# Decoder layer on one core: expansion, normalization and routing as one pipeline over batches, places looked up by matmul

## The reference

```python
x = x + state_space(layernorm(x), ...)          # a scan over 256 tokens with 16 states
x = x + align(ctx, layernorm(x))                # warping path between ctx and x; each token of x
                                                # gets the sum of the ctx rows that its path meets
x = x + moe(layernorm(x), gate, w0, w1, wo)     # below

def moe(x, gate, w0, w1, wo):                   # 4096 tokens, 64 experts, two for each token
    weights, selected = top_k(x @ gate, 2);  weights = softmax(weights)
    order = argsort(selected.reshape(-1))       # 8192 entries, grouped by expert
    xs = x[order // 2]
    h = silu(ragged_dot(xs, w0, sizes)) * ragged_dot(xs, w1, sizes)
    out = ragged_dot(h, wo, sizes)
    return sum over the two entries of a token of out * weight
```

## Time and profile before

| | us |
|---|---|
| three runs | 1441.17, 1444.8, 1447.7; median 1444.8 |
| the profiled execution | 1447.63 |
| its span | 1445.9 |
| first loop of `expand` | 773.9 to 822.7 |
| scales | 822.7 to 828.0 |
| second loop | 828.0 to 863.9 |
| `route` | 863.9 to 941.7 |
| `experts` | 941.7 to 1405.0 |
| `combine` | 1405.0 to 1445.9 |

### The profile page before, as it was taken

The page is one execution under the profiler, slowest core; times in us unless marked ns, Lnnn a source line. Parts: engine busy times, 40 slices in busy tenths (PEclk is TensorE's granted clock), DMA queues, the critical chain, the costliest instruction groups (busy, mean ns, idle before and its releaser), DMA issues. The chain is left out here.

```text
span 1445.9 us, 20750 instructions
## 1 busy us (share of the span) xinstructions
PE 995.5 (69%) x6537; PEld 901.4 (62%) x6537; DVE 946.0 (65%) x1936; ACT 583.8 (40%) x1319; POOL 631.3 (44%) x558
## 2 busy tenths in 40 slices
PE   3666877777787662776003682679999999999940
PEld 1565766767676551665003471579999998898840
DVE  1999999999999931887986767723333333233317
ACT  3668777787877642343003450512222211111100
POOL 5877787868778611000002300044454553454310
PEclk9989999999999985555556975789999999999975
DMA  6544545556565411122030034047888987888729
GB/s 197 183 142 132 173 140 178 170 144 192 142 183 169 145 33 33 30 36 53 0 116 0 8 109 159 16 123 251 281 265 276 289 281 270 270 270 262 253 70 319
DMA packets 176631, 230.00 MB, mean 159 GB/s; under 512 B 43708, under 2 KB 105676, under 8 KB 175952
## 3 DMA queue, kind: packets, MB, share of 16 engines
q1 hardware_dynamic: 156732, 205.95, 46.4%
q0 software_dynamic: 13072, 18.22, 4.2%
q10 hardware_dynamic: 6724, 4.57, 1.0%
HBM read 202.32 MB, written 22.11 MB: 155 GB/s over the span
## 5 line engine op out<-in xcount | busy, mean ns | idle before, releaser
L846 PE MATMUL st_y_ps<-ident,st_hc 128*128 128x128 f32 x2048 | 274.1, 291 | 117.3 <-DVE st_hc L489 117.3
L846 PEld LDWEIGHTS st_y_ps<-ident,st_hc 128*128 128x128 f32 x2048 | 256.7, 204 | 139.7 <-DVE st_hc L489 138.9
L371 POOL TENSOR_TENSOR st_u<-st_dx,codes 128x1024 f32<-128x1024 f32 x128 | 298.9, 2356 | 37.7 <-DVE st_h L481 36.9
L481 DVE TENSOR_TENSOR_SCAN st_h<-st_da,st_u 128x512 f32<-128x512 f32 x256 | 297.6, 1203 | 9.8 <-POOL st_u L371 9.6
L1953 PE MATMUL mo_h<-mo_xt,w 128*128 128x128 f32 (+31 forms) x2048 | 281.6, 289 | 1.7 <-DVE mo_xt L2050 1.7
L1953 PEld LDWEIGHTS mo_h<-mo_xt,w 128*128 128x128 f32 x2048 | 271.9, 193 | 7.0 <-issue 2.3
L2056 DVE TENSOR_TENSOR mo_inter<-mo_silu,mo_h 128x128 f32<-128x128 f32 (+31 forms) x256 | 75.3, 298 | 273.7 <-ACT mo_silu L2027 231.9
L2027 ACT ACTIVATE mo_silu<-mo_h 128x128 f32<-128x128 f32 (+31 forms) x256 | 72.1, 286 | 313.5 <-PE mo_h L1953 222.1
L612 ACT ACTIVATE st_da<-st_delta,st_a_neg 128x510 f32<-128x510 f32 x256 | 171.6, 685 | 66.3 <-DVE st_h L481 59.5
L1893 POOL DMA_INDIRECT outs<-mo_o,choice x95 | 99.6, 1048 | 214.6 <-DVE mo_o L2067 198.1
L489 DVE TENSOR_TENSOR st_hc<-st_h,st_cps 128x1024 f32<-128x1024 f32 x128 | 152.6, 1192 | 0.0
(11 more groups left out here) (311 smaller groups left out, 1329.1 us busy)
## 6 DMA issues: line engine op xcount, KB each, us to landing
codes<-bc SPq DMA_DIRECT2D x256, 256.0 KB, 4.0
w<-in_L_ffn_w_dram SPq DMA_DIRECT2D x128, 512.0 KB
wo<-in_L_ffn_wo_dram SPq DMA_DIRECT2D x64, 512.0 KB
co_got<-outs SPq DMA_DIRECT2D x16, 512.0 KB, 9.2
x<-in_x_dram SPq DMA_DIRECT2D x8, 512.0 KB, 8.8
st_cx<-in_ctx_dram SPq DMA_DIRECT2D x8, 512.0 KB, 4.8
dist<-st_dd SPq DMA_DIRECT2D x8, 512.0 KB, 4.9
codes<-wv_code SPq DMA_DIRECT2D x32, 128.0 KB, 3.4
```

The lines of the kernel that those rows point to most:

```text
L371: nc.gpsimd.tensor_tensor(u_sb[k % URING][:, :, :], dx[p % 2][:, :, :], over_chunks(b_sb[k % BRING]), ALU.mult).then_inc(u_ok, 1)
L481: nc.vector.tensor_tensor_scan(h_sb[k % HRING][:, dh, :], da_ps[dh][:, :], u_sb[k % URING][:, dh, :], 0.0, ALU.mult, ALU.add).then_inc(h_o ...
L846: m = nc.tensor.matmul(y_ps[t // 2][:, t % 2, dh * P:(dh + 1) * P], hc_sb[k % RING][:, dh, t * P:(t + 1) * P], K.ident[:, :], start=False, ...
```

## The change

`expand` takes in `route`; all loops over batches are written out, as beats that work on up to four batches at once.

- The spans' matrix comes from one Square in place of two Relu and a product: `apart` = (column - middle)^2, and `on` = `apart` <= `reach` (VectorE, two operations with a pointer operand).
- The scales are computed in each batch: aggregation on VectorE, Ln and Exp on ScalarE (`roots`), and seven small steps on GpSimd (`newton`).
- Turned rows are copied by ScalarE; the top two are taken from PSUM without a copy of the logits.
- In each batch VectorE makes the one-hots `hot` of both choices for two tiles, adds them and keeps running sums; TensorE gives the entries' ranks, VectorE picks and reduces them (`nth`), and TensorE turns the one-hots (`turn_marks`), copied by ScalarE.
- Behind the counts, 32 small matmuls of the turned one-hots by a table of three values for each expert (begin, room, first late place) look these up for all entries (`found_ps`); the places are computed on 64 columns.
- The table is written from 64 marks, each two operations of VectorE: `at_lo`, and `entered` with the comparison and the product in one.

GpSimd's constants for routing are written after the first `newton`. The diff, cut to its core (the removed parts are printed above):

```diff
 # ScalarE
+            def far(b):
+                if b >= 2:
+                    act.wait_ge(mask, b - 1)
+                for h in range(2):
+                    m = nc.scalar.activation(apart[b % 2][:, h, :], col[:, :], ACT.Square, bias=mid[:, h, b:b + 1])
+                m.then_inc(apart_ok, 1)
+            def roots(b):
+                u = b % 2
+                act.wait_ge(mean_ok, b + 1)
+                nc.scalar.activation(log[u][:, :], mv[u][:, :, 1], ACT.Ln, bias=eps[:, :]).then_inc(logs, 1)
+                act.wait_ge(logs, b + 1)
+                if b >= 2:
+                    act.wait_ge(scale_ok, (b - 1) * 2)
+                nc.scalar.activation(rough[u][:, :], log[u][:, :], ACT.Exp, scale=-0.5).then_inc(rough_ok, 1)
+            def normalize(b):
+                u = b % 2
+                act.wait_ge(scale_ok, b * 2 + 2)
+                ...
+                for t in range(2):
+                    m = nc.scalar.activation(xn[b % 4][:, t, :], tile(2 * b + t), ACT.Identity, bias=nmr[u][:, t:t + 1],
+                                             scale=rstd[u][:, t:t + 1])
+                m.then_inc(xn_ok, 1)
+            def take_turned(b):
+                act.wait_ge(t_ok, b + 1)
+                ...
+                nc.scalar.activation(xt[b % 2][:, :, :], xt_ps[:, :, :], ACT.Copy).then_inc(xt_ok, 1)
+            def take_marks(b):
+                act.wait_ge(ht_mm, b + 1)
+                nc.scalar.activation(hot_t[:, 2 * b:2 * b + 2, :], ht_ps[:, :, :], ACT.Copy).then_inc(ht_ok, 1)
+            for b in beats:                      # range(-2, B + 4); each step only where its batch exists
+                take_turned(b - 2); normalize(b - 1); far(b + 2); take_marks(b - 3); roots(b)
 # GpSimd
+            def newton(b):                       # seven operations on 128 x 2, from rough_ok to scale_ok
+                ...
+            for b in range(B):
+                newton(b)
+                if b == 0:
+                    routing_constants()
 # VectorE
+            for b in range(B + 4):
+                add(b); masks(b + 1); sum_up(b - 3, 1); statistics(b); largest(b - 2); aggregate(b)
+                where(b - 2); pick(b - 3); mark(b - 2); position(b - 3); choose(b - 2); sum_up(b - 2, 0)
+            ...                                  # counts, ranks, order, late places
+            dve.wait_ge(row_mm, LOOKED)
+            k = did(nc.vector.tensor_copy(found[:, :, :, :], found_ps.rearrange("p (t i c) -> p c i t", i=2, c=3)))
+            ...                                  # eight steps on 128 x 64
             for k in range(groups):
                 if k >= 2:
-                    dve.wait_ge(entered_ok, (k - 1) * MG)
-                nc.vector.tensor_tensor(at_hi[k % 2][:, :, :], places(MT), marks_of(hi, k, MT),
-                                        ALU.is_equal).then_inc(marks, 1)
-                if k >= 2:
                     dve.wait_ge(used, k - 1)
-                nc.vector.tensor_tensor(at_lo[k % 2][:, :, :], places(P), marks_of(lo, k, P),
-                                        ALU.is_equal).then_inc(marks, 1)
+                for i in range(MG):
+                    j = k * MG + i
+                    nc.vector.tensor_scalar(at_lo[k % 2][:, i, :], place[:, 0:P], lo[:, j:j + 1], None, ALU.is_equal)
+                    nc.vector.tensor_scalar(entered[k % 2][:, i, :], place[:, :], hi[:, j:j + 1], entry[:, j:j + 1],
+                                            ALU.is_equal, ALU.mult).then_inc(marks, 1)
 # TensorE
+            for b in range(B + 4):
+                expanded(b); logits(b - 2); rank(b - 3); turn_marks(b - 3); turn(b - 1)
+            ...
+            pe.wait_ge(row_ok, VALUES)
+            pe.wait_ge(ht_ok, B)
+            for t in range(TT):
+                m = nc.tensor.matmul(found_ps[:, t * 6:(t + 1) * 6], hot_t[:, t, :],
+                                     values[:, :, :].rearrange("p i c -> p (i c)"), start=True, stop=True)
+            m.then_inc(row_mm, 1)
+            for j in range(2 * TT):
+                k, i = divmod(j, MG)
+                pe.wait_ge(marks, j + 1)
+                m = nc.tensor.matmul(table_ps[:, 0:MT], at_lo[k % 2][:, i, :], entered[k % 2][:, i, :], ...)
```

More of the change, by code:

```diff
@@ L1265, in expand @@
         col = sb("ex_col", [P, L])
[L1266 to L1275, removed]
@@ L1285, in expand @@
[L1285 to L1297, removed]
@@ L1298, in expand @@
[L1298 to L1387, removed]
-                m.then_inc(top, 1)
-            def keep(b, u):
-                dve.wait_ge(top, b * 2 + 2)
-                settle(dve)
-                by_choice = lambda x: x[:, :, 0:2].rearrange("p t i -> p i t")
-                nc.vector.tensor_copy(K.top[:, :, bass.ds(b * 2, 2)], by_choice(most[u]))
-                nc.vector.tensor_copy(K.top_at[:, :, bass.ds(b * 2, 2)], by_choice(most_at[u])).then_inc(kept, 1)
-            take_turned(0, 0)
-            for u in range(4):
-                batch(0, u)
-            with dve.Fori(1, B // 4 - 1) as q:
-                for u in range(4):
-                    batch(q, u)
-            for u in range(4):
-                batch(B // 4 - 1, u)
-            keep(B - 1, 1)
@@ new lines, in expand @@
+        half = sb("ex_half", [P, 2, B])
+        size = sb("ex_size", [P, 2, B])
+        none = sb("ex_none", [P, 2, B])
+        reach = sb("ex_reach", [P, 2, B])
+        apart = ring(2, "ex_apart", [P, 2, L])
+        on = ring(2, "ex_on", [P, 2, L])
+        stats = ring(2, "ex_stats", [P, 2, 6])
+        mv = ring(2, "ex_mv", [P, 2, 2])
+        log, rough, root, near, away, rstd, nmr = (
+            ring(2, "ex_" + x, [P, 2]) for x in ("log", "rough", "root", "near", "away", "rstd", "nmr"))
@@ new lines, in _ @@
+            dve.wait_ge(constant, 7)
+            masks(0)
+            for b in range(B + 4):
+                if real(b):
+                    add(b)
+                if real(b + 1):
+                    masks(b + 1)
+                if real(b - 3):
+                    sum_up(b - 3, 1)
+                if real(b):
+                    statistics(b)
+                if real(b - 2):
+                    largest(b - 2)
+                if real(b):
+                    aggregate(b)
+                if real(b - 2):
+                    where(b - 2)
+                if real(b - 3):
+                    pick(b - 3)
+                if real(b - 2):
+                    mark(b - 2)
+                if real(b - 3):
+                    position(b - 3)
+                if real(b - 2):
+                    choose(b - 2)
+                    sum_up(b - 2, 0)
```

684 lines of the change are left out of this document (372 added, 312 removed).

## The result

The changed kernel takes 1449.09 us (median of 20 runs, 1445.05 to 1450.39), the kernel before 1443.98 us (20 runs, 1441.17 to 1449.94). The ratio is 1.003, with a 95% interval of 1.0021 to 1.0039: 5 us slower. That can be told from nothing with 20 runs each, and lies within the 0.5% that the prediction called no change.

What follows compares the result with a forecast made beforehand. The prediction took the end of routing to set the time, the experts' stage keeping its length. +25.4 - 17.4 - 1.8 = +6.2 us on the profiled 1447.63 gave 1453.8, less 2.8: 1451 us; 8 in 10 range 1438 to 1471.

Steps and rivals of the forecast that it cites:

- The two loads a batch: ScalarE's Ln and Exp in each batch: two function table loads, 32 in all, 2 x 1.30 us a batch.
- The loop: Batch period through ScalarE and GpSimd: 4.85 us of steps plus 2 x 1.30 of loads, 7.45 us.
- Part A: Routing from expansion up to the counts, 773.9 to 880.9 us before: 132.4 us against 107.0, +25.4.
- Head: Start of the batch pipeline to the first mean: 9.1 us.
- Tail: End of the batch pipeline, from roots(15): 12.4 us to the last sum, then 1.9 for last ranks, turned marks and counts.
- Part B: From the counts to the marks, 880.9 to 910.8 us before: 12.5 us in place of 29.9, -17.4.
- Part C: The marks of 64 entries, 910.8 to 939.2 us before: 26.6 us against 28.4, -1.8, ends -6 and +10.
- The sum: All of routing's changed stretches together: 25.4 - 17.4 - 1.8 = +6.2 us, forecast 1451 us.
- The first: Rival on the batch loop: one table serves Ln and Exp, period about 5.0 us, 37 us less; 1413 us, chance 0.10.
- The second: Rival: TensorE stays at half clock, pipeline at 7.6 us a batch, marks 40 us; 1469 us, chance 0.12.
- The third: Rival on the marks: VectorE's small operations overlap fully, 0.25 us per entry, marks 22.8 us; 1445 us, chance 0.15.
- The fourth: Rival on the batch loop: loads cost more than their 1.28 us, 0.75 more each being 24; 1475 to 1495 us, chance 0.05.

Runs made afterwards that it cites:

- the finer wait: Kernel before, with TensorE in the marks waiting for each ScalarE product instead of all eight of a group: 1441.49 us, ratio 0.999.
- the sets: Three groups of follow-up runs, each with the kernel before run beside it: 1425.62, 1424.02 and 1445.45 us.
- the first expectation: Expectation written for the changed kernel plus one load of a set with Ln and Exp ahead of the batches; measured 1393.3 us, ratio 0.9771.
- the one-load version: Changed kernel with the Ln and Exp set loaded ahead of the batches and again between Ln and Exp in each batch: 1412.97 us.
- the preload: Changed kernel with one line more, loading the set with both Ln and Exp ahead of the batches: 1393.3 us, ratio 0.9771.
- the version with all three edits: Changed kernel with the preload, the old marks with TensorE's wait per entry, and two GpSimd steps moved ahead of its wait: 1372.88 us, ratio 0.9639.

## Why the prediction was right, point by point

**The two loads a batch, right.** The count of two in each batch, on which the sign hung, was the author's estimate: the earlier trace rows has one load for Ln and Exp, where the set is asked for by name, and none of the rows shows the pair without that. 32 loads came, 16 in front of Ln and 16 in front of Exp, and with one the kernel is 2.3% faster than before. The runs show that the two sets differ, and not by what rule the compiler chooses them. Where the set is asked for by name, one load served all 16 pairs; without it there were two loads for each pair. Each of the changed kernel's loads cost 1.36 us in all, 1.283 of it its own length.

**The loop, right.** Predicted 7.45 us, measured about 7.35 us from one normalization to the next in the middle of the stage; with the shorter steps at both ends the 16 normalizations span 108.4 us (786.76 to 895.12), against 109.0. Its two terms hold as well: without loads 4.63 against 4.85, and 2.7 against 2.6 for the two loads.

**Part A as a whole, 2.8 us too long.** Head 8.7 against 9.1. From the first mean to the first normalization it took 4.0 us in place of 5.3 (roots 3.2 and newton 2.1): the load for Ln ran from 777.66 to 778.94 us, before the mean was there (Ln begins at 782.83), so it was hidden once. Tail from the last normalization to the key 8.6 against 9.0. With the 0.6 us of the loop, the sum is 129.6 against 132.4. The difference of +25.4 was taken from a part A of 107.0 us, which the same code also does in 104.6: measured, it is +22.6 to +25.0.

**Part B, right in kind, 3.7 us too dear.** The 32 look-ups took 1.0 us where the prediction took 5.0 and bounded them by 3.2 from below. Both came from the earlier trace rows, one matmul of 64 columns that stood alone; the listed length of one (0.17 us for each of the new ones too) says little of a row of them, which follow each other every 0.03 us. The new ones are also only 6 columns wide. No row stood behind 3.2 as the least. The rest, 7.8 us, is near the predicted 7.5.

**Part C, the wrong sign.** +2.5 in place of -1.8. The lengths 0.27 and 0.35 were right (0.280 and 0.359); the overlap of neighbours was taken as 0.11 each and was 0.08 to 0.09, which makes 0.471 an entry and not 0.39. Over 64 entries that is 5 us. Against marks whose TensorE also follows entry by entry, as the new ones do, the form costs 6.6 us; the finer wait that came with it gives 4 back, a term that the prediction did not have. Its arithmetic was also a little low: 0.27 + 0.35 less twice 0.11 is 0.40, not 0.39, and its sum then used 0.38. The nine entries that it put at half clock, at TensorE's 0.63 us, did not take longer than the others: in the kernel before with the new marks, and in the changed one, VectorE was busy for all but 0.7 us of the stretch. The earlier trace rows had already shown 21 instructions in those 5.7 us at a granted clock of 0.50. A float32 matmul shows as two (128 for the 64 entries in the marks' windows), so that is ten and a half entries, 0.54 an entry and not 0.63.

**The sum.** Part A 2.8, B 3.7 too dear, C 4.3 too cheap: 2.2 us left of 10.8. The forecast of 1451 against 1449.09 owes part of its closeness to that, which is luck: the +6.2 came out as +4.0 in the profiles, with a term of the wrong sign in it, and as +5.1 in the medians. That the stages behind routing keep their length held to within 3.4 us in the two profiles, and not between the sets (480 and 500 us).

**The rivals.** The first had its price right: 37 us predicted, 37 measured by the ratios (1.003 to 0.9771 of 1425.6), 39.5 by the traces. Its bound was named wrongly: VectorE's 4.6 us a batch turned out as 4.0, and the loop over ScalarE and GpSimd set 4.63. The second came half true: the granted clock did fall in the loop, to 0.52 from 851 to 858 us, but not for good (0.75 in the 7 us behind); and that had next to no price at this period, for the steps between normalizations stay at 7.3 to 7.5 us from 800 to 880 us. Its 7.6 us a batch, and the 7.5 and 4.2 us that the first expectation gives TensorE at half and at full clock, were the author's estimates, and no run shows them: the 24 instructions of one batch were busy 6.50 us at a granted clock of 0.52 and 3.40 us at 1.00. Its marks at 0.63 us an entry did not come either: the new ones took 0.471. The third, cheap marks, is excluded by the new marks in both kernels. The fourth is excluded by the one-load version and by the preload.

## What to carry to other kernels

When two functions alternate in a loop, as Ln and Exp here, look for the load instructions in the profile (32 of 1.283 us here, one with the set named), and name a set that has both ahead of the loop; a restructured pipeline pays off only after that, here 2.3% in place of -0.3%. An edit that moves work from three engines to one is to be priced by what one entry costs on the busiest engine after it, and 0.08 us of error there counts 64 times: two operations an entry on one engine took 30.9 us, the same work on three engines 24.3, once the last of them followed entry by entry. And where one change has several parts, time each alone; here the loads hid 37 us of gain and the marks cost 4.

## What the runs showed of the hardware

TensorE's clock changes level from batch to batch in the pipeline of the changed kernel, which repeats the same work every 7.35 us. Windows of 7 us:

```profile
844.00:851.00 7.00, 3.40 (x24) 2.67 (x23) 4.53 (x21) 5.71 (x10) 1.19 (x6) 1.00 0.11 39
851.00:858.00 7.00, 6.50 (x24) 5.06 (x24) 2.21 (x13) 5.53 (x10) 1.22 (x6) 0.52 0.11 37
858.00:865.00 7.00, 5.46 (x25) 3.96 (x24) 4.08 (x19) 5.31 (x11) 1.31 (x6) 0.75 0.11 37
```

The 24 matmul instructions of the first window are busy 3.40 us at a granted clock of 1.00, the 24 of the second 6.50 us at 0.52. In the version with all three edits, with TensorE busy 38.8 of 47 us, the granted clock is 1.00 in the whole window from 800 to 847 us. Why some stretches of the same work fall back was not settled.

32 bf16 matmuls of 128 x 128 by 6 columns took 1.02 us together at a granted clock of 0.50, 0.03 us each, though each is listed with 168 ns. VectorE's small operations with operands from pointers took 0.28 us (128 wide, one) and 0.36 us (164 wide, two), and held the engine for 0.20 and 0.27 us when they followed each other; whether the second pointer or the width makes the difference was not tried.
